# Streaming the experts' second weights in three earlier steps, and holding half of the adding stores behind them

## What is computed

```
grouped = x.reshape(b, s // g, g, d)                       # groups of 32 tokens
logits = einsum('bntd,des->bntes', grouped, Wc) + bc + tie
perm = (logits == max(logits, axis=-3)).astype(x.dtype)    # each expert takes one token per group
permuted = einsum('bntd,bntes->bnesd', grouped, perm)
inner = relu(einsum('bnesd,esdf->bnesf', permuted, W1) + b1)
result_permuted = einsum('bnesf,esdf->bnesd', inner, W2) + b2
result = einsum('bnesd,bntes->bntd', result_permuted, perm)
x = x + tanh(g_ffn) * result
```

## Time and profile before

| | |
|---|---|
| three runs | 1815.02 us median (1812.1 to 1815.61) |
| the profiled execution | 1812.23 us, its span 1810.4 us |
| TensorE busy | 1654.5 us, 91% |
| mean granted clock of TensorE | 0.965 of full |
| experts' part | from about 910 us to the end, a batch about 56 us apart |

### The profile page before, as it was taken

The page is one execution under the profiler, slowest core; times in us unless marked ns, Lnnn a source line. Parts: engine busy times, 40 slices in busy tenths (PEclk is TensorE's granted clock), DMA queues, the critical chain, the costliest instruction groups (busy, mean ns, idle before and its releaser), DMA issues.

```text
span 1810.4 us, 51743 instructions
## 1 busy us (share of the span) xinstructions
PE 1654.5 (91%) x22488; PEld 1152.1 (64%) x22488; DVE 1283.6 (71%) x1856; ACT 754.5 (42%) x995; POOL 866.3 (48%) x1016
## 2 busy tenths in 40 slices
PE   7899999999999999999778988889888898888985
PEld 4677777777777777777545664456654566545662
DVE  5677777777777777777547776577666776666766
ACT  3533232332333322322245545555455554555553
POOL 3467777767777677776323313333133331233312
PEclk9999999999999999999899999999999999999997
DMA  7534444444443544444457667786687866778656
GB/s 273 162 108 150 168 156 150 137 163 141 156 161 128 167 146 172 146 143 139 153 182 217 195 188 217 217 221 197 188 220 216 229 187 189 216 206 233 195 160 186
DMA packets 180882, 324.81 MB, mean 179 GB/s; under 512 B 23344, under 2 KB 33328, under 8 KB 179248
## 3 DMA queue, kind: packets, MB, share of 16 engines
q1 hardware_dynamic: 135728, 239.68, 41.1%
q0 software_dynamic: 17280, 31.46, 9.5%
q10 hardware_dynamic: 27648, 50.34, 8.5%
HBM read 242.71 MB, written 78.71 MB: 178 GB/s over the span
## 4 chain that ended last, share of the span: by engine, by line
PE 59%; DVE 12%; DMA 10%; issue 9%; POOL 5%; ACT 3%; ACTq 1%; SPq 1%; DVEq 0%; POOLq 0%
PE ps L1387 14%; PE ps L877 10%; PE ps L924 10%; DMA gat<-in_W 8%; PE ps L1360 7%; PE ps L937 5%; PE ps L892 3%; PE ps L950 2%; DVE mx L675 2%; PE ps L1425 2%; POOL out L1219 2%; POOL xin L184 2%; PE ps L911 2%; PE ps L1410 1%; DVE lg L679 1%
## 5 line engine op out<-in xcount | busy, mean ns | idle before, releaser
L184 POOL TENSOR_SCALAR xin<-xin,r_all,nb_all 128x512 f32<-128x512 f32 x128 | 122.0, 1129 | 502.0 <-DMA xin<-out 501.8
L1300 DVE STREAM_TRANSPOSE res<-res 128x2048 f32<-128x2048 f32 x128 | 292.0, 2295 | 0.1
L1253 ACT ACTIVATE gat<-ps 128x1536 f32<-128x1536 f32 (+1 forms) x128 | 170.7, 1344 | 208.1 <-PE ps L1360 208.1
L1316 DVE COPY res<-ps 128x1024 f32<-128x1024 f32 x128 | 156.7, 1225 | 141.3 <-PE ps L1410 141.0
L877 PE MATMUL ps<-xTh,qh 128*128 128x512 f32 x512 | 209.8, 410 | 5.5 <-DVE qs L692 1.9
L877 PE MATMUL ps<-xTh,ql 128*128 128x512 f32 x512 | 200.9, 392 | 0.0
L877 PE MATMUL ps<-xTl,qh 128*128 128x512 f32 x512 | 200.7, 392 | 0.0
L1267 ACT ACTIVATE res<-ps 128x1024 f32<-128x1024 f32 x128 | 131.1, 1025 | 155.0 <-PE ps L1410 150.6
L532 POOL TENSOR_TENSOR qc<-qc,qs 128x512 f32<-128x512 f32 x64 | 82.8, 1294 | 208.6 <-DVE qs L692 208.6
L1360 PE MATMUL ps<-sel,xin 32*128 32x128 f32 x4096 | 155.1, 290 | 26.9 <-POOL xin L184 11.5
L519 POOL TENSOR_TENSOR xTl<-xT,xTh 128x512 fp32r<-128x512 f32 x128 | 160.8, 1286 | 10.8 <-ACT xTh L575 10.8
(11 more groups left out here) (156 smaller groups left out, 3432.0 us busy)
## 6 DMA issues: line engine op xcount, KB each, us to landing
gat<-in_W ACTq DMA_DIRECT2D x192, 256.0 KB, 6.5
xT<-in_xT SPq DMA_DIRECT2D x32, 1024.0 KB, 6.0
xin<-in_x SPq DMA_DIRECT2D x64, 512.0 KB, 3.8
out<-xin SPq DMA_DIRECT2D x64, 512.0 KB, 3.6
xin<-out SPq DMA_DIRECT2D x128, 256.0 KB, 5.6
xin<-in_W SPq DMA_DIRECT2D x128, 256.0 KB, 3.4
out<-xin POOLq DMA_DIRECT2D x120, 256.0 KB, 13.5
xT<-in_W SPq DMA_DIRECT2D x68, 256.0 KB, 4.4
```

Of the source, the lines that this page charges most:

```text
L184: e.tensor_scalar(self.xn[:, t, :], self.xn[:, t, :], self.r[:, i, t:t + 1], self.nb[:, i, t:t + 1], ALU.mult, ALU.add).then_inc(self.m_xn ...
L1253: e.activation(o, v, ACT.Copy).then_inc(m_gaA.sem, 1)
L1300: e.transpose(v, v).then_inc(m_tr.sem, 1)
L1316: e.tensor_copy(o, v).then_inc(m_evV.sem, 1)
```

## The change

Unit 5 is now issued right after the eighth eviction of the gathers, ahead of all ReLUs. Unit 6 is issued between the ReLUs of the last piece (where unit 5 was), and unit 7 behind the first four `finish` (where unit 6 was). The last four `finish` issue nothing. On SP, tiles 2 and 3 of the next batch are loaded ahead of the logits instead of behind them, and GpSimd norms all four first tiles before it scales logits. GpSimd issues adding stores 0 to 3 where it did, then waits until all four quarters of unit 7 have landed, then issues stores 4 to 7. No transfer and no arithmetic is added or removed.

```diff
@@ sync @@
                 if live(i + 1):
-                    load_x(i + 1, 0)
-                    load_x(i + 1, 1)
+                    for t in range(NY):
+                        load_x(i + 1, t)
                     e.wait_ge(m_gap.sem, m_gap.at(i, 2 * C - 1))
                     route.load_logits(e, i + 1, 0)
                     e.wait_ge(m_w1.sem, m_w1.at(i, 6))
                     route.load_logits(e, i + 1, 1)
-                    for t in range(2, NT):
+                    for t in range(NY, NT):
                         load_x(i + 1, t)
@@ gpsimd @@
                 if live(i + 1):
-                    route.normed(e, i + 1, 0)
-                    route.normed(e, i + 1, 1)
+                    for t in range(NY):
+                        route.normed(e, i + 1, t)
                     route.scaled(e, i + 1, 0)
                     route.scaled(e, i + 1, 1)
-                for t in range(NY):
+                for t in range(NT):
                     if live(i - 1):
+                        if t == NY:
+                            e.wait_ge(d_room[W2_MOVED[2]].sem, d_room[W2_MOVED[2]].at(i, QUARTERS - 1))
                         add_to_out(i - 1, t)
                 if live(i + 1):
-                    route.normed(e, i + 1, 2)
-                    route.normed(e, i + 1, 3)
-                for t in range(NY, NT):
-                    if live(i - 1):
-                        add_to_out(i - 1, t)
-                if live(i + 1):
-                    for t in range(TH, NT):
+                    for t in range(NY, NT):
                         route.normed(e, i + 1, t)
@@ scalar @@
                 if live(i):
                     for n in range(2 * C):
                         copy(i, n)
+                    for c in range(QUARTERS):
+                        load_second(e, i, W2_MOVED[0], c)
                     for p in (2 * C - 2, 2 * C - 1):
                         for j in range(4):
                             hidden(i, j, p)
                             if p % 2:
-                                load_second(e, i, W2_MOVED[0], j)
+                                load_second(e, i, W2_MOVED[1], j)
                 for t in range(NT):
                     if live(i - 1) and i < B:
                         finish(i - 1, t)
-                    if live(i):
-                        load_second(e, i, W2_MOVED[1 + t // QUARTERS], t % QUARTERS)
+                    if live(i) and t < QUARTERS:
+                        load_second(e, i, W2_MOVED[2], t)
```

## The result

Over 16 runs each, the changed kernel takes 1810.17 us (1797.76 to 1815.45) and the kernel before 1819.51 us (1811.42 to 1826.92). The ratio is 0.9947, with a 95% interval of 0.9925 to 0.9968. That is about 10 us faster, where 59 were forecast. The profiled execution has a span of 1807.4 us.

A forecast was written before the change was run, and what follows sets the result against it. TensorE, busy 91% of the span, was held by short waits, chiefly for unit 7 of W2. 14 batches x 4.1 = 57 us plus 1.7 in the last: 1815.0 - 59 = 1756 us, range 1730 to 1798.

The forecast's parts named there:

- The wait for unit 7: TensorE's wait for unit 7 of W2 in the experts' part, 4.1 us in the batch read, was to go.
- The hold did no harm to the middle unit: W1's middle unit, loaded after the held stores, was to stay hidden, by 2 us in the worst case.
- Tile 7, "I take 4.0": Tile 7 of the next batch was to land at 1278, 4 us earlier, within bounds of 0 and 7.7 us.
- no real shift: Tile 4, waiting for store 0, was to land at 1266 to 1268, about when it did before.
- the overlap behind the hold: With stores 4 to 7 leaving only at 1268 to 1272, tile loads were to take 5 and 5.5 us.
- The term for tiles 2 and 3: Loading them ahead of the logits delays logits and adding stores; taken as nothing, bounds 0 and 1.5 us per batch.
- The slower work after a wait: TensorE's work at the lower clock behind the wait for unit 7, 1.2 us per batch, was to go.
- the stretch is full, and stays full: Rival, chance 0.09: tile 7 lands about when it does now, the wait becomes one for the norm; 1800 us.
- The rule that was quoted for it: All DMAs end on the same 16 engines and interleave; by that alone no reordering makes the busy stretch shorter.
- The rule on taking turns between queues: Each DMA engine alternates between queues by packet; by that alone unit 7 gains from the four held stores.
- The quarter of 3.8 us: A quarter of W2 issued at 1254.4, read as landing alone after 3.8 us, against 15.8 us with company.

The follow-up runs named there:

- x8: Changed kernel without the hold, with adding stores 4 to 7 behind the norms of tiles 4 to 7; ratio 0.997 to the kernel before.
- y2: Changed kernel with VectorE's second-half routing moved from ahead of unit 0's eviction to ahead of unit 2's; ratio 0.998 to the kernel before.
- y3: Changed kernel with unit 5 issued between the ReLUs of piece 6 instead of ahead of them; ratio 0.9982 to the kernel before.
- x1: Kernel before with only the three earlier steps of W2 (units 5, 6 and 7 issued earlier); ratio 0.9885 to the kernel before.
- y4: Kernel before with the three earlier W2 steps, and adding stores 4 to 7 between the norms of tiles 5 and 6; 1772.49 us, ratio 0.9752.
- y1: Kernel before with the three earlier W2 steps, and adding stores 4 to 7 behind the norm of tile 7; ratio 0.9808.

## Why the prediction failed

**What held.** The wait for unit 7 is gone, for the reason given: its last quarter lands 12.7 us behind the scatter's start, where it was 22.4. The wait for the norm of tile 7 is next and decides. The hold did no harm to the middle unit: SP waits there for no store.

**Tile 7, "I take 4.0", is the term that failed.** The chain is 28.6 us instead of 28.8, a shift of 0.2. Store 0 was to leave 0 to 1.5 us later; it left 5.3 us later (9.6 against 4.3). And I took 8.0 us as the least an adding store needs, from the earlier trace rows; in the changed kernel they took 3.8 at the least and 7.6 in the median. The second error cancelled most of the first: tile 4 started 14.0 us behind the scatter's start instead of 13.2 in the mean, close to "no real shift", which was right by luck.

What did not come is the shorter loads. From tile 4's issue to tile 7's landing I forecast 10.5 us (5 and 5.5) instead of 14.4; measured are 14.7 before and 13.7 in the changed kernel, in the mean. The step that failed is the overlap behind the hold: stores 4 to 7, leaving at 1268 to 1272 (13.7 to 17.7 us behind the scatter's start), were counted as out of the way of tiles 4 and 5. They left at 13.0 to 14.7 us, directly behind stores 0 to 3, and even by the forecast's own times they would have left beside tile 4, issued at 1267.5. x8 shows what that sharing costs: with these stores behind the norms the loads take 9.6 us (14.2 to 23.8) and the chain loses 3.9 us, almost the term's whole size.

**The term for tiles 2 and 3, "I take nothing, bounds 0 and 1.5 us per batch",** failed outside its bounds. The logit tiles took 4 us longer in the median, and as they left later too, the last landed 7.8 us behind the scatter's start instead of 2.3. The end of routing came 3.3 us later (12.0 behind the scatter's start against 8.7), and unit 2 waited 2.5 us per batch. I had added the two delays for each half apart, and looked for the room only on VectorE. The scaling holds GpSimd's stores too, and there nothing covers it. The runs of single parts and pairs say where the loss came from: steps alone 0.9885, steps and hold 0.9888, steps and tiles 0.9927, all 0.9947. The last two are not told apart. And y2 and y3 show that this term alone did not make the forecast fail: with the wait at unit 2 gone the batch is no shorter, since the chain holds it.

**The slower work after a wait** was forecast to go, at 1.2 us a batch. It became less, but part of it moved: in the batch shown the clock is at the lower level from 1268.0 to 1271.4, behind the wait at unit 2, and from 1281.7 to 1288.5, in and behind the second gather; before, it was from 1275.8 to 1282.6. The 1.2 us were also too small a price, as they left out the eight transposes behind unit 7, which took 1.97 us before and 1.09 in the changed kernel.

**Of the rivals,** "the stretch is full, and stays full" was the case that came, with 0.09, at 1800 us; 1815.02 x 0.9947 is 1805. Its sentence, that the wait is turned into one for the norm, describes x1, y2 and y3 exactly. As a law it is too strong. The same traffic in another order (y4) shortens the chain by 3.4 us. The rule that was quoted for it, from the Trainium skill, "DMA: Bandwidth & Descriptors", section "Issuing engines are not separate DMA queues", holds here for the sum: the three queues took 59.1% of 1810.4 us, 1070 us of all engines, before, 59.3% of 1807.4, 1072 us, in the changed kernel and 60.3% of 1774.9, 1070 us, in y4. The order decided who waited for it. The rule on taking turns between queues (the Trainium skill, same page, section "Queues, rings and completion order") fits too, as the logit tiles on SP's queue slowed down from 4.0 to 8.0 us beside ScalarE's quarters. The quarter of 3.8 us in the earlier trace rows was not alone, as the prediction says, but one of three issued within 1 us.

**What stays open.** In the fourteen traces store 0 leaves, in the mean of each, between 4.3 and 9.8 us behind the scatter's start, but lands at 12.5 to 14.7 us. What holds this landing was not isolated, and it, not the issue, starts tile 4. Nor is it shown what TensorE's gaps without a releaser in y1 are; they came with stores that ran beside the first layer.

## What to carry to other kernels

When a stretch has every DMA engine busy, a transfer that is moved forward lands on whatever was quiet there: list all transfers within its new 5 us, and for each who waits, on every engine and not only on the one being helped. If one wait hides another that is as late, compute both ends of the batch (here path and chain) for every edit; only the larger one pays. A hold must name the transfers it protects: on top of the earlier steps, holding stores 4 to 7 until unit 7 had landed added nothing (0.9888 against 0.9885), while placing them behind the norms of tiles 4 and 5 was worth some 1.3% (0.9752).

## What the runs showed of the hardware

The time of a 256 KB transfer to land moved by a factor of about two with the order of the issues, at the same total traffic: adding stores had a median of 13.5 us before and 7.6 in the changed kernel, logit tiles 4.0 and 8.0. A smallest value over 120 transfers (8.0 us) was no floor: others took 3.8. And the length of a wait alone did not tell whether TensorE's clock fell behind it: in the changed kernel it fell behind 1.91 us of idling at 1096.6 and 3.46 us at 1266.8, but stayed at 1.00 behind 2.79 us at 1324.1, where unit 3's 32 matmuls took 1.14 us instead of 2.01.
